# A relational graph layer on one core: four tiles of the second half fetched by matmul in every turn, not in every other turn

## The reference

```python
h = feat[src]
for r, w_r in enumerate(weight):
    m = m + (etypes == r)[:, None] * (h @ w_r)
out = segment_sum(m, dst, num_segments=3125)
x = layernorm(x + out)
```

## Time and profile before

| | |
|---|---|
| median of 3 runs | 776.13 us (774.11 to 776.22) |
| the profiled execution | 776.07 us |
| its span, from the first to the last instruction | 774.3 us |
| TensorE busy | 698.0 us, 90% |
| TensorE weight loads | 673.4 us, 87% |
| VectorE busy | 661.0 us, 85% |
| ScalarE busy | 635.1 us, 82% |
| GpSimd busy | 549.9 us, 71% |
| mean granted TensorE clock | 0.976 |

### The profile page before, as it was taken

The page is one execution under the profiler, slowest core; times in us unless marked ns, Lnnn a source line. Parts: engine busy times, 40 slices in busy tenths (PEclk is TensorE's granted clock), DMA queues, the critical chain, the costliest instruction groups (busy, mean ns, idle before and its releaser), DMA issues.

```text
span 774.3 us, 25434 instructions
## 1 busy us (share of the span) xinstructions
PE 698.0 (90%) x8821; PEld 673.4 (87%) x8822; DVE 661.0 (85%) x2221; ACT 635.1 (82%) x1232; POOL 549.9 (71%) x588
## 2 busy tenths in 40 slices
PE   1888999999999999999899998999999899999955
PEld 1578999999999999999898998989899898989955
DVE  4998798889989888898988899898898989899824
ACT  5866898988889898888979889888888879888713
POOL 2665677777777777777777777777777777777760
PEclk9979999999999999999999999999999999999985
DMA  8321333322332232233222222223223222222211
GB/s 206 89 73 53 73 70 77 80 74 73 79 81 72 74 79 80 66 82 78 68 78 81 65 82 78 72 74 81 72 74 78 80 66 82 76 70 65 54 51 43
DMA packets 29950, 59.01 MB, mean 76 GB/s; under 512 B 11624, under 2 KB 11874, under 8 KB 29930
## 3 DMA queue, kind: packets, MB, share of 16 engines
q0 software_dynamic: 18368, 37.65, 18.4%
q1 hardware_dynamic: 11254, 20.29, 10.0%
q10 hardware_dynamic: 308, 0.80, 0.5%
HBM read 56.30 MB, written 2.40 MB: 76 GB/s over the span
## 4 chain that ended last, share of the span: by engine, by line
POOL 62%; issue 24%; DVE 6%; PE 4%; DMA 1%; ACT 1%; POOLq 1%; ACTq 0%; DVEq 0%
POOL rows L324 61%; DVE pick L522 3%; PE own L747 3%; POOL rows L320 2%; DMA x_sb<-in_x 1%; DVE onehot L589 1%; PE own L891 1%; DVE outT L631 0%; PE agg L782 0%; DMA rows<-x_parts,gidx 0%; DVE x_sb L663 0%; POOLq L76 0%; ACT pick L414 0%; DVE src_f L577 0%; DVE src_f L579 0%
## 5 line engine op out<-in xcount | busy, mean ns | idle before, releaser
L324 POOL DMA_INDIRECT rows<-x_parts,gidx x558 | 529.1, 948 | 194.8 <-issue 174.0
L747 PE MATMUL own<-xp,pick 125*128 125x192 bf16 x5800 | 503.2, 248 | 44.0 <-ACT pick L414 21.0
L747 PEld LDWEIGHTS own<-xp,pick 125*128 125x128 bf16 x5800 | 482.1, 99 | 62.4 <-issue 50.3
L522 DVE TENSOR_SCALAR pick<-src_h,node 125x516 bf16<-125x516 f16 (+1 forms) x1240 | 465.8, 455 | 39.0 <-ACT src_h L376 38.9
L408 ACT ACTIVATE away<-src_h,node_neg 125x516 bf16<-125x516 f16 (+1 forms) x310 | 195.1, 692 | 1.8
L414 ACT ACTIVATE pick<-away,one 125x516 bf16<-125x516 bf16 (+1 forms) x310 | 194.6, 692 | 0.0
L589 DVE TENSOR_SCALAR onehot<-ramp,krel 128x112 bf16<-128x112 bf16 x806 | 148.8, 261 | 0.0
L782 PE MATMUL agg<-onehot,rows 128*128 128x112 bf16 x2418 | 133.4, 214 | 13.1 <-DMA rows<-x_parts,gidx 12.0
L782 PEld LDWEIGHTS agg<-onehot,rows 128*128 128x128 bf16 x2418 | 124.2, 99 | 18.2 <-issue 15.9
L423 ACT ACTIVATE rows<-own 128x384 bf16<-128x384 f32 x124 | 58.2, 470 | 89.6 <-PE own L747 89.3
L388 ACT ACTIVATE aggT<-agg 64x512 f32<-64x512 f32 x124 | 72.7, 586 | 14.5 <-PE agg L782 13.0
(11 more groups left out here) (66 smaller groups left out, 83.3 us busy)
## 6 DMA issues: line engine op xcount, KB each, us to landing
src_b<-in_src SPq DMA_DIRECT2D x62, 258.0 KB
rows<-x_parts,gidx POOLq DMA_INDIRECT x574, 2.5
x_parts<-xp SPq DMA_DIRECT2D x1, 728.0 KB
x_parts<-xp SPq DMA_DIRECT2D x1, 672.0 KB
out<-x_sb SPq DMA_DIRECT2D x2, 224.0 KB
x_sb<-in_x ACTq DMA_DIRECT2D x1, 364.0 KB
x_sb<-in_x ACTq DMA_DIRECT2D x1, 336.0 KB
src_i<-in_src SPq DMA_DIRECT2D x1, 312.0 KB
```

The source lines that it names most:

```text
L324: pool.indirect_dma_start(rows[:, u, j, :], None, x_parts, bass.IndirectOffsetOnAxis(ap=gidx[:, u, j:j + 1], axis=0)).then_inc(rows_in[u] ...
L522: v.tensor_scalar(pick[u][:, b, 0:CUT * cut_width(u, odd)], src_h[u][:, :, 0:cut_width(u, odd)], node[:, b:b + 1], None, ALU.is_equal).the ...
L747: return nc.tensor.matmul(own_slot(u, h), pick[u][:, b, h * P:(h + 1) * P], xp[:, b, 0:SPLIT, :].rearrange("p s d -> p (s d)"), start=(b = ...
```

## The change

The second half's first four tiles are now products in every turn. Before, they were products in odd turns, and in even turns (0, 2, ... 30, sixteen of them) three were products and the fourth was a gather.

```diff
         def own_count(u, odd):
 
-            return OWN[u] if u == 0 or odd else FEWER
+            return OWN[u]
```

## The result

The changed kernel takes 789.87 us (median of 4 runs, 788.51 to 790.00), the kernel before 775.12 us (median of 4). The ratio is 1.0188 with a 95% interval of 1.0163 to 1.0212: slower by 14.7 us. The forecast was 793.2 us in a range of 787 to 799.

What follows compares the result with a forecast made beforehand. TensorE and ScalarE waiting for each other bound the early turns, GpSimd's gathers the later ones. After the change, turn 30 starts at 756.7 us; plus 34.7 for the end and 1.8 around the span gives 793.2 us, range 787 to 799.

Steps and rivals of the forecast that it cites:

- Two regimes: Kernel before: its own pace, 44.98 us for two turns, until turn 12 starts; then GpSimd's gathers, 46.2 us.
- The ring: TensorE's products and ScalarE's take_pair and act_picks wait for each other, setting the early pace of 44.98 us for two turns.
- The sum for two turns: Changed kernel's four turn parts: 12.56 + 11.18 + 12.56 + 11.04 = 47.34 us, over GpSimd's 45.0.
- wide part 3: Last part of ScalarE's act_picks ahead of an even turn takes 1.95 us instead of 1.62.
- The end: From the start of turn 30: no gather waits, so 34.7 us to the span's end instead of 42.7.
- VectorE's cover: VectorE's wider picks in odd turns end before the next turn's start with 2.2 us to spare.
- The signs: Profile after: even turns of 23.6 and 23.7 us, TensorE waiting about 0.8 us for ScalarE, GpSimd 1.2 us per turn.
- the start: Up to turn 2: VectorE's picks add 1.39 us, so turn 2 starts at 93.92 us; range -1.4 to +1.6.
- GpSimd as the lasting bound: Rival: gathers run without a gap to the end and the change gains, 756 us; chance 0.04.
- slack in the ring: Rival: wide turns use slack between TensorE and ScalarE, two turns take about 46.1 us, about 776 us; chance 0.04.
- VectorE giving way: Rival: VectorE stalls turn starts by 0.5 us per turn, 14 us more, about 807 us; chance 0.07.

Runs made afterwards that it cites:

- e1_drop_fourth: Kernel before, with the fourth tile's sixteen even-turn gathers left out from turn 2 on and nothing in their place: 755.96 us, ratio 0.976.
- e6_before_cut32: Kernel before, with ScalarE's five blocks cut into parts of 3 and 2 instead of 2 and 3: 774.80 us, ratio 1.0.
- e4_cut32: Changed kernel, with ScalarE's five blocks cut into parts of 3 and 2 instead of 2 and 3: 769.23 us, ratio to before 0.9934.
- e5_cut32_early: e4_cut32, with ScalarE doing part 2 of act_picks before take_pair(i, 1, 1) instead of behind it: 757.16 us, ratio to before 0.9784.
- e3_drop_matmuls: e1_drop_fourth plus only TensorE's part of the change, 25 more matmuls in even turns, picks kept narrow: 783.31 us, ratio 1.0108.
- e2_drop_wide: e1_drop_fourth plus only the wider picks on ScalarE and VectorE, still three products in even turns: 759.73 us, ratio 0.9803.
- e8_spare8: Changed kernel, with eight more unused compares per turn on VectorE ahead of the second half's picks: 819.48 us, ratio 1.0585.
- e9_before_both: Kernel before, with both edits of e5_cut32_early, on a chip where the kernel before took 1343.12 us: 1311.06 us, ratio 0.9759.
- e11_before_both: e9_before_both run again, on a chip where the kernel before took 1370.11 us: 1351.73 us, ratio 0.9856.

## Why the prediction was right

*Two regimes, and GpSimd's pace in the second.* Shown: with one gather less in even turns and nothing in its place the kernel falls to 755.96 us (`e1_drop_fourth`), and a looser ring alone changes nothing (`e6_before_cut32`). The border was placed a little early: 337.99 is the end of turn 12, as A(13) is at 338.95, and A(12) to A(14) still took 362.21 - 317.13 = 45.08 us. The forecast's sum does not use it.

*The ring.* The forecast read from coinciding ends that TensorE and ScalarE wait for each other. `e4_cut32` and `e5_cut32_early` show it: the same work in other pieces and another order takes 20.6 and 32.7 us off the changed kernel's 789.87.

*The sum for two turns, 47.34 us.* It measured 47.31 on average. Its two parts were right too. For the matmuls it had 2.02 us by the turns' lengths (12.56 against 10.54; 2.06 by the blocks' lengths), and `e3_drop_matmuls` measured 2.02; for the wide part 3 it had 0.33, and `e2_drop_wide` measured 0.33.

*The end, 34.7 us after A(30).* It measured 34.75. The gather waits of 6.07 and 1.84 us are gone. Part of this is the gather itself: in `e1_drop_fourth`, without the added matmuls, one such wait of 2.26 us was left.

*VectorE's cover of 2.2 us.* It was 2.4.

*The signs.* Turns of 23.73 and 23.60 us came (23.7 and 23.6 forecast), with waits of 0.84 and 0.69 us at A (about 0.8 forecast) and 1.3 us per turn on GpSimd (1.2 forecast); no wait for a gather is left on TensorE.

*What was off: the start.* A(2) was forecast at 93.92 us and came at 89.67 in the profiled execution, 4.2 us early, which is the whole difference of the spans (791.4 and 786.7, but for 0.4). This term missed its own range of -1.4 to +1.6 us. The term of 1.39 us for VectorE's picks was right: they took 7.85 us. These are the changed kernel's rows that answer to the earlier trace rows:

```profile
33.23 7.85 DVE L522 TENSOR_SCALAR pick<-src_h,node 125x516 bf16<-125x516 f16 x20
...
54.88 8.42 PE L747 MATMUL own<-xp,pick 125*128 125x192 bf16 x100 [0.39 <-DVE pick L522]
...
66.07 8.42 PE L747 MATMUL own<-xp,pick 125*128 125x192 bf16 x100 [2.77 <-ACT pick L414]
```

0.92 us came from the inputs: VectorE waited 7.2 instead of 8.1 us for the transfer of `src_i` in the first 17 us, and started these picks at 33.23 instead of 34.15. The other 3.3 us are the two products of 100 matmuls at E(0) and A(1), 8.42 us each instead of 10.08 and 10.07. Their windows show the clock, first before, then after the change:

```profile
54.40:67.20 12.80, 10.08 (x100) 9.68 (x100) 10.07 (x33) 7.29 (x16) 5.18 (x6) 0.87 0.15 40
67.20:81.50 14.30, 13.87 (x157) 13.42 (x158) 10.31 (x34) 10.51 (x21) 8.48 (x9) 0.88 0.23 61
```

```profile
54.90:66.00 11.10, 8.40 (x100) 8.17 (x100) 10.02 (x33) 8.85 (x18) 6.57 (x7) 1.00 0.25 73
66.00:80.00 14.00, 13.57 (x173) 13.40 (x174) 11.27 (x39) 11.84 (x23) 9.43 (x10) 1.00 0.27 64
```

Before, a part of each was granted 1.2 instead of 2.4 GHz. The full clock does not need the change: `e1_drop_fourth` has TensorE's start of before and took 8.43 and 8.42 us, after waits of 2.65 and 2.77 us that are no shorter than those of the earlier trace rows; `e2_drop_wide` and `e3_drop_matmuls` took 8.42 and 10.08. So it varies between executions of one start, and the forecast took it from one execution as if it belonged to the kernel. Whether the change has a part in it is not shown: at E(0) all six kernels up to `e8_spare8` with the 25 further matmuls in turn 0 took 8.42 or 8.43 us, and of the four without them two took 10.07 or 10.08; at A(1) both lengths occur with them and without them. The other three runs of the changed kernel have spans of 788.0 to 788.2 us at a mean clock of 0.986, the profiled one 786.7 at 0.988, about one such product's difference; the forecast was 3.3 us above the median and 4.7 above the profiled execution.

*The rivals.* GpSimd as the lasting bound, slack in the ring and VectorE giving way are all refuted for the changed kernel, the last one only up to 2.4 us: `e8_spare8` is what it looks like. The rule that the most occupied engine is the bottleneck (the Trainium skill, Perfetto Trace Analysis, section Identifying the Most-Contended Engine) would have given 809 us. The traces disagree: TensorE's share was 90% before (87% by its weight loads), the highest of all engines, and it waited in both regimes. In `e5_cut32_early`, where TensorE is busy 44.79 of 45.09 us, it fits; but GpSimd, the last by busy time with 71%, is as near to its limit there.

## What to carry to other kernels

When the chain of waits runs through one engine, look for a stretch in which that engine is not the bound, since it shows the pace of everything else; work moved off the bound is worth only the distance between the two paces, and here the move cost more (2.3 us for two turns) than that distance (1.2). When two engines hand work back and forth, time the piece between one engine's last result and the other's next start, not their busy shares: cutting ScalarE's five blocks 3 and 2 instead of 2 and 3, and filling its wait with a block of work that needed no result, turned a kernel 1.9% slower than before into one 2.2% faster (that these two edits gain nothing without the change is argued, as said above). Take times in a start-up stretch from several executions.

## What the hardware showed beside

TensorE's clock during the first 80 us differs between executions of one program's start: the products of 100 matmuls at E(0) and A(1) took 8.42 us with a granted clock of 1.00, or 10.08 with one of 0.87 (`e1_drop_fourth` and before), and 8.41 to 8.43 in all the later turns that are shown here of runs up to `e8_spare8`.

Two chips ran the kernel before 1.73 and 1.77 times slower (1343.12 and 1370.11 us), and only TensorE was behind: in `e9_before_both` and `e11_before_both` a gather still took 948 and 947 ns, and a group of 20 wide picks 7.87 us, but TensorE's matmuls came in ones and twos with 0.4 to 1.9 us between them after the first 66 or so of a block. In `e11_before_both` the granted clock was 1.00 during those 66 (610.98 to 616.60) and 0.65 in the broken stretch behind (616.60 to 629.20), so the gaps began at full clock; over the whole run it was 0.785. The profile gives no releaser for these gaps ("issue"), and what makes them is open.
